# Two cross-attention layers on one core: natural and transposed scores of two heads issued side by side, one in each half of TensorE's rows

## The reference

```python
# layer 0 (77 text tokens, 179 image tokens), per sequence
q = x @ Wq;  k, v = text @ Wk, text @ Wv;  ki, vi = ip @ Wk_ip, ip @ Wv_ip
text_out = softmax(q_h k_h^T / 4) v_h                       # per head
sem = (softmax(q k^T / 4) text) ip^T / 4                    # once for all heads
ip_out = softmax(q_h ki_h^T / 4 + 0.5 * sem) * mask @ vi_h  # per head
x = (text_out + ip_out) @ Wout + bout + x
# layer 1 (252 text tokens, 4 image tokens): the same, but sem is per head,
# of the l2-normed (softmax(q_h k_h^T / 4) text) with the l2-normed image tokens
```

## Time and profile before

| | |
|---|---|
| median of 3 runs | 1666.56 us (1665.37 to 1671.36) |
| span of the profiled execution | 1665.6 us, first to last instruction; its own time is not listed apart, and the runs lie from 0 to 6 us above this span |
| PE / PEld / DVE busy | 1599.7 / 1424.2 / 1376.6 us (96 / 86 / 83% of the span) |
| ACT / POOL busy | 992.3 / 844.8 us (60 / 51%) |
| DMA | 175.31 MB, about a third of the 16 engines' time |
| natural scores, line 265 | 1280 matmuls, 300.1 us busy |
| transposed scores, line 278 | 1280 matmuls, 259.9 us busy |

### The profile page before, as it was taken

How to read it: one execution, slowest core, us unless ns; L and a number is a source line. 1 busy time by engine, 2 the same in 40 slices (tenths; PEclk the granted TensorE clock), 3 DMA queues, 4 the chain that set the end, 5 groups by cost and what they waited for, 6 DMA issues and landing times.

```text
span 1665.6 us, 42402 instructions
## 1 busy us (share of the span) xinstructions
PE 1599.7 (96%) x14248; PEld 1424.2 (86%) x14248; DVE 1376.6 (83%) x3937; ACT 992.3 (60%) x2044; POOL 844.8 (51%) x789
## 2 busy tenths in 40 slices
PE   6999999999999999998989999999999999999986
PEld 5888888888888888788878998989998989998866
DVE  4688788888888888867879998999999998998874
ACT  3455565555556555655656666666666666666651
POOL 3224422222222323424767676777667776777662
PEclk9999999999999999999999999999999999999988
DMA  8334444444444444542323332333233323332201
GB/s 223 97 105 121 129 121 124 124 129 125 120 129 124 124 128 122 144 123 75 112 88 87 100 95 80 102 106 99 66 109 102 100 67 101 101 103 63 79 22 43
DMA packets 204225, 175.31 MB, mean 105 GB/s; under 512 B 45441, under 2 KB 203531, under 8 KB 204011
## 3 DMA queue, kind: packets, MB, share of 16 engines
q1 hardware_dynamic: 204010, 172.60, 35.8%
HBM read 112.13 MB, written 60.38 MB: 104 GB/s over the span
## 4 chain that ended last, share of the span: by engine, by line
PE 88%; DVE 6%; issue 3%; DMA 1%; SPq 1%; ACT 1%; POOL 0%; DVEq 0%; POOLq 0%; ACTq 0%
PE MISC L103 26%; PE GP L103 20%; PE NAT L265 10%; PE TR L278 8%; PE PV L324 5%; PE PV L309 4%; PE PV L306 3%; PE PV L327 2%; PE MISC L227 2%; PE MISC L367 1%; DVE ZP L895 1%; PE MISC L368 1%; PE MISC L466 1%; DVE TMP L779 1%; PE MISC L388 1%
## 5 line engine op out<-in xcount | busy, mean ns | idle before, releaser
L540 ACT ACTIVATE P<-TA 128x512 f32<-128x512 f32 x320 | 202.6, 633 | 279.4 <-DVE TA L888 278.0
L984 POOL TENSOR_TENSOR ZS<-ZP 128x256 f32<-128x256 f32 x267 | 255.4, 957 | 210.4 <-DVE ZP L895 209.0
L265 PE MATMUL NAT<-KS,QS 65*128 65x256 f32 x1280 | 300.1, 317 | 3.6 <-DMA KS<-qk_parts 2.1
L103 PE MATMUL GP<-PH,GH 128*128 128x256 f32 (+1 forms) x960 | 248.8, 288 | 20.9 <-DVE ZP L895 19.9
L278 PE MATMUL TR<-QS,KS 69*128 69x256 f32 (+1 forms) x1280 | 259.9, 285 | 4.6 <-DMA QS<-max_rows 2.5
L783 DVE TENSOR_REDUCE MX<-NAT 128x2 f32<-128x504 f32 x320 | 216.6, 677 | 51.3 <-PE NAT L265 46.9
L901 DVE SCALAR_TENSOR_TENSOR PM<-P,PH 128x512 f32<-128x512 f32 x320 | 255.3, 798 | 0.0
L215 POOL TENSOR_TENSOR PARTS<-QKF,PARTS 112x508 fp32r<-112x508 f32 (+3 forms) x93 | 119.3, 1283 | 265.1 <-ACT PARTS L568 263.2
L265 PEld LDWEIGHTS NAT<-KS,QS 65*128 65x128 f32 x1280 | 201.2, 192 | 56.9 <-issue 42.1
L103 PE MATMUL GP<-PH,GL 128*128 128x256 f32 (+1 forms) x960 | 243.0, 281 | 0.0
L543 ACT ACTIVATE P<-TR 128x512 f32<-128x512 f32 x320 | 192.7, 602 | 74.3 <-PE TR L278 71.3
(11 more groups left out here) (253 smaller groups left out, 3886.9 us busy)
## 6 DMA issues: line engine op xcount, KB each, us to landing
QS<-qk_parts SPq DMA_DIRECT2D x480, 64.0 KB
KS<-qk_parts SPq DMA_DIRECT2D x480, 64.0 KB
qk_parts<-PARTS SPq DMA_DIRECT2D x128, 224.0 KB, 2.8
CT<-in_ctx_t SPq DMA_DIRECT2D x32, 512.0 KB, 3.9
qk_parts<-PARTS SPq DMA_DIRECT2D x64, 192.0 KB, 2.4
XT<-in_x_t SPq DMA_DIRECT2D x48, 112.0 KB, 2.6
XT<-x_t SPq DMA_DIRECT2D x48, 112.0 KB, 2.4
XB<-in_x SPq DMA_DIRECT2D x16, 320.0 KB, 4.1
```

What stands on the lines that cost most here:

```text
L103: ins = e.matmul(out, lhs, rhs, start=(n == 0), stop=(n == len(pairs) - 1))
L265: ins = e.matmul(NAT[s % 2][:, i * T:(i + 1) * T], QS[0:KQ, h, i * 128:(i + 1) * 128], KS[0:KQ, h, :], start=True, stop=True)
L540: e.activation(P[:, s % NP, :], TA[:, s % 2, :], ACT.Exp, scale=SCALE).then_inc(q["exp"], 1)
L984: e.tensor_tensor(ZS[s % NZ][:, :], ZP[:, s % 2, 0:S], ZP[:, s % 2, S:2 * S], ALU.add).then_inc(q["zs"], 1)
```

## The change

The stacks get a second buffer and a second place. QS and KS become [128 partitions, 2 buffers, 10, 256]: the buffer is that of the sequence (b % 2), and an even head lies on partitions 0 to 51, an odd head on partitions 64 to 115. The rows of zeros go away: the rows of maxima follow the 48 stack rows at once (KM = 48), so the natural scores read 48 partitions, and the transposed ones 52 (layer 0) or 50 (layer 1). As LEAD is 11, the natural head t + 11 and the transposed head t of a slot are of different parity. Their matmuls are issued in turn: natural 0, transposed 0, natural 1, transposed 1, behind the waits of both. Around that:

- A group's stack is written by twelve DMAs of 32 KB in place of six of 64 KB; the row of maxima by two DMAs in place of one; the selecting rows by two DMAs in place of one at the start, and in layer 1 for two sequences (20 DMAs) in place of one (5).
- The stack's wait is for the transposed scores of two sequences before.
- The two clearing memsets and SP's and PE's waits for them go.

```diff
-KQ, KM = 65, 65
-STACKS = 2 * len(Q_PARTS)
+KM = 16 * len(Q_PARTS)
+HALF_PE = 64
+STACKS = 4 * len(Q_PARTS)
...
-    QS, KS = sb("QS", [TRK0, H, S], F32R), sb("KS", [TRK0, H, T], F32R)
+    QS, KS = sb("QS", [128, 2, H // 2, S], F32R), sb("KS", [128, 2, H // 2, T], F32R)
...
+    def of_head(s, rows):
+
+        b, h = divmod(s, H)
+        r0 = HALF_PE * (h % 2)
+        return QS[r0:r0 + rows, b % 2, h // 2, :], KS[r0:r0 + rows, b % 2, h // 2, :]
...
-            s = t + LEAD
+            s, r = t + LEAD, t
             if 0 <= s < 2 * S1:
...
-                for i in range(2):
-                    ins = e.matmul(NAT[s % 2][:, i * T:(i + 1) * T], QS[0:KQ, h, i * 128:(i + 1) * 128],
-                                   KS[0:KQ, h, :], start=True, stop=True)
-                ins.then_inc(q["nat"], 1)
...
-                tr_free(e, s)
-                w = TRK0 if b < B else TRK1
-                for i in range(2):
-                    ins = e.matmul(TR[s % 2][:, i * S:(i + 1) * S], KS[0:w, h, i * 128:(i + 1) * 128],
-                                   QS[0:w, h, :], start=True, stop=True)
-                ins.then_inc(q["tr"], 1)
+            if 0 <= r < 2 * S1:
+                if r % HG == 0:
+                    e.wait_ge(q[f"mrow{r // HG % 2}"], mrows(r // HG))
+                if r == 0:
+                    e.wait_ge(q["sel"], 32)
+                tr_free(e, r)
+            for i in range(2):
+                if 0 <= s < 2 * S1:
+                    qs, ks = of_head(s, KM)
+                    ins = e.matmul(NAT[s % 2][:, i * T:(i + 1) * T], qs[:, i * 128:(i + 1) * 128], ks, start=True, stop=True)
+                    if i == 1:
+                        ins.then_inc(q["nat"], 1)
+                if 0 <= r < 2 * S1:
+                    qs, ks = of_head(r, TRK0 if r < S1 else TRK1)
+                    ins = e.matmul(TR[r % 2][:, i * S:(i + 1) * S], ks[:, i * 128:(i + 1) * 128], qs, start=True, stop=True)
+                    if i == 1:
+                        ins.then_inc(q["tr"], 1)
...
-        e.memset(KS[0:KQ, :, :].bitcast(F32), 0.0).then_inc(q["clear"], 1)
...
-        e.memset(QS[0:KQ, :, :].bitcast(F32), 0.0).then_inc(q["clear_q"], 1)
...
-                    e.dma_start(dst[16 * r:16 * r + 16, h0:h1, :].bitcast(F32),
-                                parts_h[b % 2, i, parts[r], D * h0:D * h1, :].rearrange("(h d) t -> d h t", d=D)).then_inc(q[f"stack{hg}"], 16)
+                    src = parts_h[b % 2, i, parts[r], D * h0:D * h1, :].rearrange("(j a d) t -> a d j t", a=2, d=D)
+                    for half in range(2):
+                        r0 = HALF_PE * half + 16 * r
+                        e.dma_start(dst[r0:r0 + 16, b % 2, 2 * hg:2 * hg + 2, :].bitcast(F32), src[half]).then_inc(q[f"stack{hg}"], 16)
...
+                for half in range(2):
+                    r0 = HALF_PE * half + KM
+                    src = rows.rearrange("part grp (j a i) q -> part grp a j (i q)", j=2, a=2)[:, 0:n, half, :, :]
+                    e.dma_start(QS[r0:r0 + 2 * n, b % 2, 2 * hg:2 * hg + 2, :].bitcast(F32),
+                                src.rearrange("part grp j q -> (part grp) j q") if n == 2 else src[:, 0, :, :]).then_inc(q[f"mrow{g % 2}"], 16)
...
-                if b:
-                    e.wait_ge(q["tr"], HG * (g - NGRP) + HG)
+                if b >= 2:
+                    e.wait_ge(q["tr"], HG * (g - 2 * NGRP) + HG)
```

More of the change, by code:

```diff
@@ L77, in stacked @@
 def stacked(b):
-    return 16 * STACKS * b + (16 if b > B else 0)
+    return 16 * STACKS * b + 32 * min(max(b - B, 0), 2)
 def mrows(g):
-    return 16 * (g // 2 + 1)
+    return 32 * (g // 2 + 1)
 class Ring:
@@ L192, in build @@
     q = semaphores(nc, ctx, "w_q w_k w_v w_o w_rest sel x_in c_in xn_in spilled0 spilled1 spilled2 stack0 stack1 stack2 stack3 stack4 "
-                   "mrow0 mrow1 mxw0 mxw1 store store_t fill clear clear_q w_hi w_lo xt_hi xt_lo ct_hi ct_lo qk qk_f qk_hi qk_lo "
+                   "mrow0 mrow1 mxw0 mxw1 store store_t fill clear w_hi w_lo xt_hi xt_lo ct_hi ct_lo qk qk_f qk_hi qk_lo "
                    "tl tpm texp tp tpt tpts g0 g0s snm sn stm st vm v nat mx nh nm tr sum exp pv pvs ont on "
@@ L252, in _ @@
                 ins.then_inc(q["stm"], 1)
-            s = t + LEAD
+            s, r = t + LEAD, t
             if 0 <= s < 2 * S1:
-                b, h = divmod(s, H)
                 if s == 0:
                     e.wait_ge(q["w_rest"], 3 * 16)
[L258 to L261, removed]
+                if s % HG == 0:
+                    e.wait_ge(q[f"stack{s // HG % NGRP}"], stacked(s // H + 1))
@@ L1123, in _ @@
         e.wait_ge(q["sel_h"], 32)
-        e.dma_start(KS[KM:TRK0, :, :].bitcast(F32), sel_h[0:4, :].unsqueeze(1).broadcast_to([4, H, T])).then_inc(q["sel"], 16)
-        e.wait_ge(q["clear"], 3)
-        e.wait_ge(q["clear_q"], 1)
+        for r0 in (0, HALF_PE):
+            e.dma_start(KS[r0 + KM:r0 + TRK0, :, :, :].bitcast(F32).rearrange("p b j t -> p (b j) t"),
+                        sel_h[0:4, :].unsqueeze(1).broadcast_to([4, H, T])).then_inc(q["sel"], 16)
         for t in range(T0, T1):
@@ L1135, in _ @@
             if g is not None:
[L1136 to L1141, removed]
+                b, hg = divmod(g, NGRP)
+                n = 2 if g < G1 else 1
+                e.wait_ge(q[f"mxw{g % 2}"], 16 * (g // 2 + 1))
+                rows = rows_h[g % 2].rearrange("(part grp c) q -> part grp c q", part=2, grp=2)
+                for half in range(2):
[3 more added lines that the diff above has]
+                                src.rearrange("part grp j q -> (part grp) j q") if n == 2 else src[:, 0, :, :]).then_inc(q[f"mrow{g % 2}"], 16)
             g = due_group(t, -4 * HG)
@@ L1146, in _ @@
                     e.wait_ge(q[f"spilled{m}"], 32 * (b + 1))
-                if b:
-                    e.wait_ge(q["tr"], HG * (g - NGRP) + HG)
+                if b >= 2:
+                    e.wait_ge(q["tr"], HG * (g - 2 * NGRP) + HG)
                 stack(b, hg)
-                if b == B:
-                    e.dma_start(KS[KM:TRK1, HG * hg:HG * hg + HG, :].bitcast(F32),
-                                sel_h[4:6, :].unsqueeze(1).broadcast_to([2, HG, T])).then_inc(q[f"stack{hg}"], 16)
+                if b in (B, B + 1):
+                    for r0 in (0, HALF_PE):
+                        e.dma_start(KS[r0 + KM:r0 + TRK1, b % 2, 2 * hg:2 * hg + 2, :].bitcast(F32),
+                                    sel_h[4:6, :].unsqueeze(1).broadcast_to([2, 2, T])).then_inc(q[f"stack{hg}"], 16)
             for m in range(3):
```

## The result

The changed kernel takes 1828.71 us, the median of 4 runs (1820.55 to 1838.81), against 1666.12 before in the same comparison: 1.0974 times as long, 95% interval 1.0931 to 1.1018. It is 162 us slower, where 64 were forecast.

The account below looks back on a forecast made before the run. PE was taken as the bound throughout, DVE 9% behind in layer 1. Pairs and passages 63 + 3, stack DMAs 10, start 5, idle taken in -17 gave +64 us: 1730 us, this case 1700 to 1765, whole range 1640 to 1855.

Parts of the forecast that it names:

- Twice the stack DMAs: SP's queue: double issues make the maxima's readback 0.7 us late in a layer 0 group; taken as 10 us.
- bound of 56: Layer 0: upper cost of the late readback if each of 80 groups loses 0.7 us.
- Common waits: PE: the natural pair now stands behind the transposed pair's waits; costed at nothing.
- Passage and pairs: PE: passages into and out of half-rows cost 0.40 us a slot, pairs save 0.236; 0.164 more between whole-array work.
- 63 + 3 - 17: PE: 63 us for slots with both pairs, 3 for single-pair slots, less 17 of idle taken in.
- idle time that a slower PE was to take in: PE's waits for DVE's ZP and maxima, 34 us; half absorbed by longer slots: -17 us, between 0 and -34.
- 600 forecast: PE's loader: idles with the word "issue" before line 265's loads and before what follows, some 600 times each.
- Start: Start of the kernel: six more stack DMAs and a later first readback, +5 us, between 0 and 8.
- The first: Rival on PE: half-rows need no passage, 1580 us; milder, emptying with loads going ahead, 1640 us; chance 0.22.
- third: Rival on PE: no passage, but the halves take turns, so only DMAs and start count; 1670 to 1675 us, chance 0.05.
- The second: Rival on PE: halves load one after the other, 1859 us, or second pair's load uncovered, 1797 us; chance 0.15.
- The fourth: Rival in layer 0: the maxima's readback decides, 56 us in place of 10, 1776 us; chance 0.08.

Follow-up runs that it names:

- experiment 3: Changed kernel with LEAD = 13 in place of 11, the natural scores 13 slots ahead: 1829.34 us.
- experiment 7: Kernel before with one part at a time: only the stacks in twelve DMAs a group, 1721.52 us; only the readback of the maxima in two DMAs, 1668.62 us.
- experiment 1: Kernel before, whole-array matmuls, with twelve stack DMAs of 32 KB and the readback of the maxima split into two: 1793.36 us.
- experiment 8: Readback of the maxima issued by ACT, stacks left on SP: changed kernel 1725.81 us; kernel before with stacks in twelve DMAs 1683.85 us.
- experiment 6: experiment 2 with both natural matmuls issued before both transposed ones: 1747.20 us.
- experiment 4: Kernel before without the rows of zeros: matmuls read 48 and 52 (layer 1: 50) rows from partition 0, none paired: 1834.17 us.
- experiment 9: experiment 2 with the pairs of two slots issued together: in even slots 1739.96 us; with odd slots in layer 0 1758.43 us.
- experiment 2: Changed kernel with layer 0's stacks in two pieces, 24 DMAs a sequence in place of 60, none between maxima write and readback: 1748.63 us.

## Why the prediction was wrong

The direction and the mechanism of the pairs were right. The step that failed is the term **Twice the stack DMAs**: taken as 10 us, bounded at 56, measured at about 120 (the later start is in that figure). The prediction held that SP is not full and that a late readback costs each group at most 0.7 us; the runs showed a queue with no room over a whole period, whose lateness passes on from group to group.

*Twice the stack DMAs.* Two differences of runs give its size: after minus the same with its readback out of the queue, 1828.7 - 1725.8 = 103 us, for a readback behind twelve stacks; and 1683.9 - 1667.3 = 17 us for the split stacks where they have no lead. The text said that SP itself was not full, since in the earlier trace rows it was through with a group after 4 us of 9. That was one group. The sum over 20 slots was to be had from the same trace: SP issues for 58% of 43.1 us, 25.0. Thirty more stack DMAs at 0.42 (in the mean of layer 0 they take 0.48) make at least 12.6, five more readbacks at 0.32 make 1.6, together 39.2, and some 90 issues with 0.05 between them 4.5 more: 43.7 us in a time of 43.1, so the room was gone. That a split readback takes 1.26 us, not twice 0.32, shows only in the trace after; with it the sum is 47, and experiment 3, with no wait left on SP, shows 48.7. So the queue alone holds layer 0 back by 4 to 5.6 us in each of 16 sequences, 64 to 90 us; part of that the longer slots of the pairs would have taken anyway. The bound of 56 priced one late issue against the room of one group; a full queue passes its lateness on to the next group, which is why the parts of experiment 7 don't add.

The Trainium skill, "Perfetto Trace Analysis", What "DMA-bound" means, counts the issuing engine's sequencer, solid with DMA slices, among the things that can bound. The trace agrees: SP is solid in the rows above, while the core's 16 DMA engines are busy for 36 to 38% of layer 0, less than the 42 to 43% of before.

*Common waits: about nothing, as forecast.* In experiment 1 the natural pair still goes ahead of the wait for the readback, and 20 slots of layer 0 take 50.3 us; the 0.9 that the pairs cost there (below) make 51.2, and after takes 51.3.

*A second price of the same wait.* Nothing in the forecast allowed for the clock. Three stretches of PE after, in layer 0 (start:end, length, busy and count, granted clock, DMA):

```profile
500.00:510.00 10.00, 7.38 (x45) 0.82 0.28 83
510.00:520.00 10.00, 10.00 (x79) 0.84 0.47 134
520.00:530.00 10.00, 10.00 (x92) 1.00 0.41 114
```

In the first PE stands for 2.6 us, and the granted clock is 0.82; in the second PE is never idle but does 79 matmuls at 0.84. Both figures are means: the clock stood at 1.2 GHz (0.51 in the row of 506.3 to 513.2 us, 35 matmuls) from where PE started again, and at 2.4 before and after. In 100 to 400 us after, the clock is 0.92. At the rate of the version of experiment 8 with pairs (5286 matmuls in 590.0 busy us of 100 to 700, 0.112 each, clock 0.99) the 2279 matmuls take 254 us; they took 273.6. So, if the mix of matmuls is the same, some 20 us of that stretch go to matmuls that are longer, beside the 21 more in which PE stands.

*Passage and pairs: right in the mechanism, near in the sum.* From the last whole matmul to the second one behind the pairs are 0.20 + 0.22 + 0.22 + 0.22 = 0.86 us (experiment 6 and the timeline after), where six steps of 0.118 made 0.71: +0.15, forecast +0.164. In time, the two versions of experiment 8 differ by the pairs (and by what comes with them: the second buffer, the memsets left out, and the readback's second issue, on ACT): 1725.8 - 1683.9 = 42 us, where 63 + 3 - 17 = 49 were forecast. By the counts it is 0.9 us for 20 slots in layer 0 and 1.5 in layer 1, 14 + 24 us, and the rest at the ends. That the sum comes so near is partly luck. The idle time that a slower PE was to take in is still there: with pairs in experiment 8 PE waits 18.9 us for ZP, against 19.9 in the earlier trace rows, and the loader's waits for the maxima are 24.5 us in place of 13.8. So the passages and the pairs cost about 42, not 66. The loader's idles before the natural pair are 443 with 113.7 us there, and 448 with 184.7 us after, fewer than the 600 forecast; the transposed pairs have next to no idle under that word (1.7 us after). The text also took it from the earlier trace rows that PV's four matmuls take no longer than one; 0.22 us is nearly two steps of 0.118, and no row shows one alone. That halves do work at once is shown by the pairs themselves.

*Start: too small.* The first transposed matmul came 12 us later, forecast 5 (0 to 8); in both versions with ACT's readback it is 3, so the rest is the same queue's.

*The rivals.* The first and third need half-rows to have no passage, or its loads to be covered; experiment 4 and the timelines show a passage in full. The second needs partners some 0.1 us apart, or each pair's load behind the matmuls before it; partners start within 10 ns, and in experiment 9 later pairs follow after 0.12. The fourth named the place, the readback in layer 0, and its sign, and was given 0.08; its price was half of what came.

*What stays open.* In experiment 2 SP is at 58%, and 20 slots of layer 0 take 45.5 us, some 1.4 more than with ACT's readback and twelve stacks a group. There no stack stands between a write of the maxima and its readback, but SP waits for the write to land, and the write can stand behind a string of stacks. SP's own wait for that landing is 173.5 us in 110 to 740 us, in 68 times, the longest 5.4. In 30 of the 80 groups the transposed pair goes within 2.4 us of the readback's issue, as against 1 with ACT's readback. So PE still meets late readbacks there; that they are the 1.4 us was not tried.

## What to carry to other kernels

Before doubling DMAs on one queue, sum its issue times over a whole period of the loop, the gaps between them included, and compare with the period: 4.7 us of issues were free where the queue stood at 58%, and cost 4.6 where it was full. Then look which DMA of that queue has the least time to spare, and take that one out of the line; here moving a 1.26 us issue to another engine gave back 103 us. Two half-row matmuls at once save one step of 0.118 us, but going in and out cost 0.39 (0.86 less four steps); two pairs in a row don't repay that, and four only just would (0.47), if nothing else waits for them.

## What the runs showed that was not expected

- Issue time on SP doesn't follow size: 0.41 us for a stack of 64 KB and for one of 32 KB (0.48 and 0.47 in the mean of 100 to 690 us, before and after); and the readback, split in two, takes 0.6 for each half where the whole took 0.32.
- Matmuls of different row halves start out of program order. In experiment 6 the first transposed one (1304.63) starts 0.21 us ahead of the second natural one (1304.84) that was issued before it. The Trainium skill, "TensorE: Matmul & The Clock Gate", Part 3, What overlaps and what doesn't, has matmuls strictly in program order; the measurement differs here.
